# Attention of a two-block kernel: V products issued in pairs of rounds, with a ring of 18 exponentials in two places

## The reference

```python
h = _layernorm(x, axis=-1) * (1 + ca) + sa
x = x + ga * _L0_attn_ref(h, L0_attn_Wq, L0_attn_Wk, L0_attn_Wv, L0_attn_Wo)
...
x = x + gb * _L0_ffn_ref(...)      # then a second block with a mixer and an MLP
```

## Time and profile before

| what | us |
|---|---|
| median of 3 runs | 752.07 (750.55 to 754.78) |
| the profiled execution, its own time | 754.48 |
| its span, first to last instruction | 752.7 |
| TensorE shown busy | 711.7 (95%) |
| VectorE, ScalarE, GpSimd shown busy | 472.8, 318.0, 314.6 |
| head 3 of the attention, first product to first product of the next | 30.26 |

### The profile page before, as it was taken

How to read it: one execution, slowest core, us unless ns; L and a number is a source line. 1 busy time by engine, 2 the same in 40 slices (tenths; PEclk the granted TensorE clock), 3 DMA queues, 4 the chain that set the end, 5 groups by cost and what they waited for, 6 DMA issues and landing times.

```text
span 752.7 us, 10280 instructions
## 1 busy us (share of the span) xinstructions
PE 711.7 (95%) x3718; PEld 429.2 (57%) x3718; DVE 472.8 (63%) x716; ACT 318.0 (42%) x536; POOL 314.6 (42%) x254
## 2 busy tenths in 40 slices
PE   4998899999999999889999999999979999999998
PEld 1444333433333342148787888654548788877886
DVE  3787677788888886236865557788875433338211
ACT  3311266667677777751325401463343223223100
POOL 0325673755566565771447333226322212125300
PEclk9999799999999999999999999999989999999999
DMA  8347516252260200330013200204100111011111
GB/s 308 106 127 224 123 44 166 73 123 48 78 123 18 39 3 9 94 99 28 29 57 98 71 0 1 77 30 87 70 0 1 57 56 55 29 56 59 41 70 43
DMA packets 24111, 53.00 MB, mean 70 GB/s; under 512 B 4252, under 2 KB 8100, under 8 KB 23044
## 3 DMA queue, kind: packets, MB, share of 16 engines
q1 hardware_dynamic: 24068, 52.44, 24.6%
HBM read 45.63 MB, written 6.60 MB: 69 GB/s over the span
## 4 chain that ended last, share of the span: by engine, by line
PE 79%; DVE 10%; issue 4%; DMA 2%; ACT 2%; SPq 2%; POOL 1%; DVEq 0%; ACTq 0%; POOLq 0%
PE ps L869 76%; DVE mxp L1812 2%; DMA rq<-in_mask 1%; PE ps L886 1%; DVE st L1654 1%; DVE xnb L1678 1%; ACT pr L1458 1%; PE ps L1053 1%; DVE rt L1693 1%; PE ps L1121 0%; SPq L719 0%; DVE x L1896 0%; DVE qsw L1863 0%; DMA q_parts<-parts 0%; POOL arena L2357 0%
## 5 line engine op out<-in xcount | busy, mean ns | idle before, releaser
L869 PE MATMUL ps<-arena 128*128 128x512 f32 (+1 forms) x1404 | 326.3, 392 | 1.9 <-DVE arena L1697 1.2
L869 PEld LDWEIGHTS ps<-arena 128*128 128x128 f32 (+1 forms) x1404 | 259.4, 186 | 60.4 <-DVE arena L1697 1.9
L1812 DVE TENSOR_REDUCE mxp<-ps 128x2 f32<-128x1024 f32 (+3 forms) x160 | 172.8, 1115 | 44.2 <-PE ps L869 43.6
L1458 ACT ACTIVATE pr<-ps 128x512 f32<-128x512 f32 x288 | 162.0, 596 | 75.5 <-PE ps L869 71.6
L869 PE MATMUL ps<-Qst,Kst 99*128 99x512 bf16 x288 | 100.2, 389 | 6.1 <-ACT pr L1458 4.8
L869 PE MATMUL ps<-Kst,Qst 96*128 96x512 bf16 (+3 forms) x384 | 98.3, 333 | 5.4 <-DVE mxp L1812 4.2
L2258 POOL TENSOR_TENSOR pr<-pr,cap 128x512 int32<-128x512 int32 x56 | 71.1, 1284 | 38.0 <-ACT pr L1458 38.0
L869 PE MATMUL ps<-pr,vr 128*32 128x512 f32 x576 | 76.5, 604 | 0.0
L869 PEld LDWEIGHTS ps<-Qst,Kst 99*128 99x128 bf16 x288 | 24.4, 98 | 79.6 <-ACT pr L1458 64.0
L869 PEld LDWEIGHTS ps<-Kst,Qst 96*128 96x128 bf16 x384 | 36.4, 99 | 51.3 <-DVE mxp L1812 20.2
L2357 POOL TENSOR_TENSOR arena<-raw,arena 128x1024 fp32r<-128x1024 f32 x11 | 26.2, 2391 | 81.0 <-ACT arena L1532 80.2
(11 more groups left out here) (203 smaller groups left out, 833.6 us busy)
## 6 DMA issues: line engine op xcount, KB each, us to landing
wmr<-in_wmr SPq DMA_DIRECT2D x8, 1280.0 KB, 10.6
raw<-in_w SPq DMA_DIRECT2D x16, 512.0 KB, 3.2
Qst<-q_parts SPq DMA_DIRECT2D x42, 128.0 KB
q_parts<-qparts SPq DMA_DIRECT2D x3, 768.0 KB, 4.9
x<-in_x SPq DMA_DIRECT2D x8, 256.0 KB, 5.9
wm<-in_wm SPq DMA_DIRECT2D x4, 512.0 KB, 7.5
raw<-in_up SPq DMA_DIRECT2D x8, 256.0 KB, 2.6
raw<-in_down SPq DMA_DIRECT2D x8, 256.0 KB, 2.6
```

Source lines behind the costliest of these rows:

```text
L869: return nc.tensor.matmul(outp, lhs, rhs, start=start, stop=stop, skip_group_check=True)
L1458: A(pr[:, k % PRING, :], ps[:, 4 + k % 2, :], ACT.Exp, scale=float(DH) ** -0.5).then_inc(exp_done, 1)
L1812: V.tensor_reduce(mxp[:, kh, g0:g0 + heads, i].rearrange("p (b e) -> p b e", e=per), units, AXX, ALU.max)\
```

## The change

In `head_body` of TensorE two V rounds are issued together behind T11, T19, T27 and T35 (rounds 0 and 1, 2 and 3, 4 and 5, 6 and 7), in place of one behind T7, T11 and every fourth product from there; round 8 stays behind T1 of the next head. The ring grows from 12 to 18 places: the first 12 stay where they were, the other 6 lie in the space of the first transposed layer norm. A small function gives the place of exponential k, and TensorE, ScalarE and GpSimd use it.

```diff
-PRING = 12
+PRING, PR_LOW = 18, 12
...
-        pr = at("pr", [P, PRING, D], F32, HT_B)
-        ot = at("ot", [P, 2, D], F32, HT_B + PRING * 2048)
+        pr_low = at("pr_low", [P, PR_LOW, D], F32, HT_B)
+        pr_high = at("pr_high", [P, PRING - PR_LOW, D], F32, ACT_B + 40 * 1024)
+        ot = at("ot", [P, 2, D], F32, HT_B + PR_LOW * 2048)
...
+        def exps(k):
+            s = k % PRING
+            return pr_low[:, s, :] if s < PR_LOW else pr_high[:, s - PR_LOW, :]
...
-                    last = mm(ps[q:q + 32, 6 + i // 4, :], vr[:, j, :], pr[:, k % PRING, :], j == FIRST_J[i],
+                    last = mm(ps[q:q + 32, 6 + i // 4, :], vr[:, j, :], exps(k), j == FIRST_J[i],
                               j == LAST_J[i])
...
                     t_unit(n, k)
-                    if k % 4 == 3 and k > 4:
+                    if k % 8 == 3 and k > 4:
+                        pv_round(n, k // 4 - 2)
                         pv_round(n, k // 4 - 1)
...
-                    A(pr[:, k % PRING, :], ps[:, 4 + k % 2, :], ACT.Exp, scale=float(DH) ** -0.5).then_inc(exp_done, 1)
+                    A(exps(k), ps[:, 4 + k % 2, :], ACT.Exp, scale=float(DH) ** -0.5).then_inc(exp_done, 1)
...
-                    v = pr[:, k % PRING, :].rearrange("p (g t) -> p g t", g=G).bitcast(I32)
+                    v = exps(k).rearrange("p (g t) -> p g t", g=G).bitcast(I32)
```

## The result

The changed kernel takes 771.45 us (767.72 to 773.18, 4 runs) where the kernel before takes 751.48 (750.55 to 754.78, 4 runs): a ratio of 1.0244, with a 95% interval of 1.0203 to 1.0285, or 15 to 21 us more (the medians alone stand 19.97 us apart, within that). Slower was forecast; the 765.4 us were too few, and the median lies 1.5 us above the range of 760 to 770. The profiled execution is the shortest of the four, 767.72 us, which happens to meet the 767.8 that the sum gave for it. That meeting is luck in good part, as the stretches show.

What follows compares the result with a forecast made beforehand. The prediction took TensorE, nearly all in the matmul helper, to bound the kernel. Lost wait cover summed to 13.3 us, putting the profiled execution at 767.8 and the median at 765.4, with its own range 760.5 to 769.5.

Steps and rivals of the forecast that it cites:

- Slower was forecast: Whole kernel: slower given chance 0.85, faster 0.10, same 0.05; median forecast 765.4 us.
- the 767.8 that the sum gave: Whole kernel: profiled execution, counted at 754.48 us, plus 13.3 us lost, makes 767.8.
- The price of the waits: Four places per full head: 0.85 for the added round less what TensorE gains where one stood; 1.92 us lost.
- the bound of 3.2 us in its favour: Turn of the maxima: if T26 followed T25 by the full 0.46, seven heads would save 3.2 us (762.2).
- The two bounds and the spread: Total: 762.2 if the maxima turn gains, 766.5 if more score units wait; run spread -1.5, +2.7 us.
- The saving of the switch: Each pair of V rounds: second round 0.85 against 1.09 us, saving 0.24 of TensorE; 7.7 us over 32 pairs.
- The rival that carried it through to 744 us: Whole kernel: TensorE never held up, the 7.7 us of switches come back, 744.4 us; chance 0.10.
- the last head's term: Last head, exponential loop only: eight products and rounds 5.90 us against 5.78; 0.12 lost per pair, 0.5 over four.
- the clock rival: Heads: new stalls lower TensorE's clock, one head at half speed costing up to 30 us, 780 or more; chance 0.04.
- the forecast's own sign of being wrong: Attention heads: a granted clock under 1.00 between 95 and 340 us, among the listed signs of a wrong forecast.
- the sum of 13.3: All heads: 9.6 us for heads 1 to 5, 1.52 head 0, 1.68 head 6, 0.5 last head.
- The ring: Exponentials: 18 places cost nothing either way; with 12, exponential 20 would have waited for a round behind T19.

Runs made afterwards that it cites:

- the first four experiments: Ring of 18 alone, 752.76 us; pairs alone with ring of 12, 770.10; pairs only where score units stand, 765.06; pairs only in the bare loop, 759.32.
- the filler ahead of head 0: Kernel before with 12 matmuls more, and a wait for their bank, ahead of its attention heads: 751.23 us, ratio 0.9982.
- the units moved: Changed kernel with score units and the turn of the maxima moved to where the single rounds stood: 765.98 us, ratio 1.0155 to the kernel before.

## Why the prediction was right, and where it was not

- **The price of the waits held.** Head 3 from T0 to T12, to T20, to T28 and to the next T0, before and after:

```profile
181.20:192.05 10.85, 10.43 (x74) 4.14 (x70) 8.88 (x12) 7.93 (x14) 5.67 (x7) 1.00 0.85 163
192.05:198.43 6.38, 6.34 (x42) 2.17 (x39) 5.53 (x6) 4.44 (x8) 3.72 (x4) 1.00 0.20 85
198.43:204.76 6.33, 6.33 (x54) 2.31 (x50) 5.11 (x11) 4.55 (x8) 2.69 (x3) 1.00 0.01 3
204.76:211.46 6.70, 6.70 (x52) 2.86 (x49) 5.47 (x6) 4.45 (x8) 6.25 (x6) 1.00 0.02 5
...
183.07:194.32 11.25, 10.53 (x74) 4.24 (x71) 9.10 (x11) 7.92 (x14) 6.53 (x6) 1.00 0.93 194
194.32:201.03 6.71, 6.27 (x42) 2.18 (x39) 5.22 (x5) 4.44 (x8) 3.57 (x3) 1.00 0.04 15
201.03:208.28 7.25, 6.56 (x54) 2.46 (x50) 5.17 (x10) 4.55 (x8) 2.63 (x4) 1.00 0.01 3
208.28:215.36 7.08, 6.64 (x53) 2.89 (x49) 5.28 (x5) 4.45 (x8) 5.59 (x5) 1.00 0.03 6
```

  Place by place that is 0.40, 0.33, 0.92 (0.86 in the heads beside it) and 0.38, where 0.39, 0.32, 0.85 and 0.36 were forecast. The turn of the maxima gives back nothing at all, as was assumed, so the bound of 3.2 us in its favour was idle. (The two bounds and the spread that the forecast names give 760.7 to 769.2; it wrote 760.5 to 769.5.)
- **The saving of the switch held, and did not reach the end.** The second round of a pair costs 0.85, as read from the last two rounds of before. What the 0.24 less consists of, no run here shows. The rival that carried it through to 744 us failed in all four places.
- **The step that failed is the last head's term, and with it the clock rival.** The text priced the bare loop at "0.12 lost per pair, 0.5 over four", and gave a drop of the clock a chance of 0.04, since "the last head kept 1.00 with TensorE idle for 4.7 of 27.34 us". The share of idle time was the wrong thing to compare. Before, no stretch between two rounds held more than four products; after, eight, of which the last six each wait. In the changed kernel's profiled execution the clock falls there and nowhere else from 84 us to the end of the heads, it does so with pairs in the bare loop alone, and a filler that takes the idle time away brings it back. That is the forecast's own sign of being wrong, a clock under 1.00 between 95 and 340 us. Why one group is caught and the next is not stays open. The rival's price was mis-sized too: not 30 us for a head, but 1.1 to 1.6 us for each group of rounds that is caught, some 4 to 5 in all. Pairs in the bare loop cost 5.6 us where 0.6 was forecast for them; with these 5.0 the sum of 13.3 becomes 18.3, inside the measured 15 to 21. That 751.48 times the ratio gives 18.3 as well is chance to the tenth: the 5.6 alone has an interval of 3.3 to 7.3.
- **The Trainium skill's section on cycling PSUM banks** ("A second HAM failure mode: psum-queue depth-cycling" of "TensorE: Matmul & The Clock Gate") says that short pauses while PSUM banks are cycled can make the clock swing. It was set aside because the kernel before cycled two banks at full clock. The changed kernel cycles the same two banks and does swing (0.61, 1.00, 0.56 in the first three stretches shown), so the trace now agrees with it.
- **The ring was rightly costed at nothing, for a reason half wrong.** With 12 places exponential 20 would not have waited either: T20 itself stands behind the pair on TensorE. The pairs with the ring of 12 show it.
- **Executions differ by a stretch that the sum took for fixed.** The profiled execution of before had half clock from 84 to 94 us. The runs of that kernel beside the first four experiments were granted 0.995 to 0.997 over the span where they took 750 us, and 0.989 to 0.991 where they took over 754; the filler ahead of head 0 points to this stretch as the difference, without proving it run by run. Head 0's merge of the maxima differs too: it is shown 0.19 us long in the profiled executions of both kernels, and 1.85 and 2.10 with pairs in the bare loop alone and with the units moved. A difference added to such a median carries an error of up to 4 us, one reason why the profiled executions are 13.2 us apart and the medians 20.0.

## What to carry to other kernels

Work that looks like it interrupts a tuned order may be what covers its waits: before moving it, read for each instruction behind it when its bank or slot really comes free, and count only the difference as gained. The second round was 0.24 us cheaper wherever a pair ran at full clock, 29 of 32 places, and yet each place in a full head lost 0.3 to 0.9 us. Where TensorE is left alone with a loop that waits on another engine, look at the granted clock of short stretches, not of the whole head; useless matmuls there can be cheaper than the clock they keep.

## What the runs showed of the hardware that was not expected

- Idle time too short to matter in itself lowers the granted clock: two products of the bare loop take 1.08 us, of which 0.44 is their own issue, and eight products in a row brought a fall to half clock in three of five groups of the changed kernel; the same loop broken by a round every four products kept 1.00.
- 32 more matmuls made a head shorter (28.70 against 31.09 us) by keeping the clock.
- A second float32 round in the four strips costs 0.85 us where a single one costs 1.09; it was read at the end of the kernel before and again in every pair of head 3 and in the full-clock stretch at 319 us.
